# Scores from three bf16 parts on 96 rows a head, in place of two f32r parts on 96 rows for two heads

## The chip, the core and the metric

The kernel runs on one core of a Trainium2 chip. The metric is device time in microseconds of one execution, the median of the runs. Five engines work side by side: TensorE (PE, its weight loads are written PEld), VectorE (DVE), ScalarE (ACT), GpSimd (POOL) and SyncE (SP), which here only issues DMAs. They meet at semaphores; each engine works through its own list in order.

## What is computed

A transformer block on x of 2 batches x 1024 positions x 256 features: attention with 16 heads of 16 features, then a mixture of 8 low-rank maps, each with a residual and a layer norm behind it. Cut to what the change touches:

```python
Q = split_heads(Xn @ Wq + bq)
K = split_heads(Xn @ Wk + bk)
scores = jnp.einsum('bhqd,bhkd->bhqk', Q, K) / jnp.sqrt(jnp.float32(D_HEAD))
scores = jnp.where(causal, scores, jnp.float32(-jnp.inf))
A = jax.nn.softmax(scores, axis=-1)
AV = jnp.einsum('bhqk,bhkd->bhqd', A, V)
```

All inputs and outputs are float32, and the inputs are drawn so that scores are large, so q and k must enter the scores with nearly their full precision.

## The kernel before

The program is one list of events (`program_order`), and each engine walks through the list and emits its own share of every event. The list is written by hand and by a small planner (`attention_order`): for each of 2 batches, 4 groups of 4 heads, 2 chunks of 512 queries.

**Projections.** Event `qk` (one of 8 a batch: 2 chunks x 2 halves of the features x q or k): PE multiplies (L691), ACT writes the value rounded to f32r, the high part, to `qk` (L473), DVE writes value minus high, the low part (L562).

**Stacks.** Event `stack` (16 in all, one for each group and chunk): SP issues six DMAs (L388) that lay parts of q and k out in `stq` and `stk`, so that one product over 96 rows gives high x high + high x low + low x high. One `stk` tile serves two heads (`PAIRS`): the rows of the other head meet zeros in `stq`, which POOL writes once (L410, L424). There are three sets of stacks. The fourth group of a batch waits until the first group's value products have read the first set. Order on SP is order in the list: groups 1 and 2 (24 DMAs) stand in one block behind the row copy of group 0, chunk 0, and ahead of that of group 0, chunk 1.

**Maxima.** Event `max`: PE computes scores with queries on the partitions (L736), on the diagonal it adds a mask by a bf16 product (L740), DVE reduces a bank to maxima (L582). `split` makes two f32r parts of the maxima (L591 to L596), `rows` turns them on PE (L746), DVE moves them to `mrow` (L604), and SP copies them as two more rows below `stq` (L399), where `stk` has -1. So the scores proper come out with their row's maximum taken off.

**Scores and values.** Event `score`: PE computes 128 keys x up to 512 queries of one head over 98 rows (L758), ACT takes the exponential (L483), POOL clears above the diagonal (L448). Event `value` (one a step, behind four scores): eight products of 32 columns of weights (L778). A step is four scores and one `value`, with two to four maxima of a later block between them. Maxima and projections pass through 4 banks of PSUM that DVE (and ACT) free, scores through 3 banks that ACT frees.

The first scores of a chunk wait for that chunk's row copy. The residual, the layer norms and the mixture (L685, L691, L788, L823) are woven in by `program_order`.

## Time and profile before

| | us |
|---|---|
| runs | 511.52, 509.01, 509.17 |
| median | 509.17 |
| span of the profiled execution | 510.6 |
| PE busy | 454.6 (89%) |
| PEld busy | 265.5 (52%) |
| DVE busy | 324.8 (64%) |
| ACT busy | 218.8 (43%) |
| POOL busy | 71.0 (14%) |

The profile names only the span of its execution; it lies between the runs, 1.4 us above their median. Busy times of PE overlap a little, since matmuls are pipelined: from start to start is the time that one takes in a stream. L12 is line 12 of the kernel. A bracket at the end of a timeline's row is idle time of that engine ahead of it, and what ended it. The batches divide the span: layer norm and projections of batch 0 to about 43 us, its attention to about 230, projections of batch 1 and the mixture of batch 0 to about 290, attention of batch 1 to about 460, then the last mixture.

### The profile page before, as it was taken

Reading aid. Unit: us, or ns where it says so; the run is one execution under the profiler, and the core shown is the slowest. Engines: PE = TensorE matmul, PEld = TensorE weight load, DVE = VectorE, ACT = ScalarE, POOL = GpSimd, SP = SyncE. Lnnn points to the kernel's source line nnn. Section 1 sums busy time; section 2 is a strip of 40 time slices with the busy share of each in tenths; the row PEclk is TensorE's granted clock in tenths of the full one; section 3 lists DMA queues with packets and bytes.
Section 4 is the critical chain, followed back from the end, with each engine's and each line's share of the span. In section 5 each row is a group of like instructions: output and inputs, shape, how many; then the busy total and the mean of one; then the engine's idle time right before and its main releaser. Section 6 shows DMA issues by size and latency. Waiting matters only on the chain.

```text
span 510.6 us, 6947 instructions
## 1 busy us (share of the span) xinstructions
PE 454.6 (89%) x2512; PEld 265.5 (52%) x2512; DVE 324.8 (64%) x780; ACT 218.8 (43%) x470; POOL 71.0 (14%) x97
## 2 busy tenths in 40 slices
PE   0289799999999999999899995999999999999693
PEld 0145565556546554357557752555655554447352
DVE  6936588678778674526476894478868855114276
ACT  1132034666666756333421131466666757532110
POOL 9720010022011010100400010012102001010000
PEclk9999699999999999799999997699999999999897
DMA  5006990025002000000423195006100000000011
GB/s 165 0 10 108 213 161 7 3 46 83 3 0 85 2 2 1 0 1 3 117 66 62 36 168 89 1 3 112 15 1 2 3 2 1 0 1 1 0 42 42
DMA packets 13266, 21.18 MB, mean 41 GB/s; under 512 B 2352, under 2 KB 9776, under 8 KB 13232
## 3 DMA queue, kind: packets, MB, share of 16 engines
q1 hardware_dynamic: 13232, 20.73, 19.5%
q8 instruction: 20, 0.33, 0.3%
q14 instruction: 14, 0.11, 0.1%
HBM read 5.78 MB, written 2.10 MB: 15 GB/s over the span
## 4 chain that ended last, share of the span: by engine, by line
PE 77%; DVE 12%; ACT 4%; DMA 2%; issue 2%; SPq 2%; DVEq 0%; ACTq 0%
PE ps L691 24%; PE ps L758 18%; PE ps L778 15%; PE ps L736 13%; PE ps L740 3%; DVE mx L582 3%; DVE nv L521 2%; PE ps L685 2%; ACT pr L483 2%; SPq L388 1%; PE ps L788 1%; DVE st L533 1%; DMA stq<-mrow 1%; DVE x L540 1%; PE ps L823 1%
## 5 line engine op out<-in xcount | busy, mean ns | idle before, releaser
L483 ACT ACTIVATE pr<-ps 128x512 f32<-128x512 f32 (+3 forms) x384 | 171.7, 493 | 164.4 <-PE ps L758 162.6
L582 DVE TENSOR_REDUCE mx<-ps 128x1 f32<-128x512 f32 (+3 forms) x304 | 185.3, 655 | 58.9 <-PE ps L740 40.7
L758 PE MATMUL ps<-stq,stk 98*128 98x512 f32 (+3 forms) x384 | 146.0, 414 | 11.8 <-DMA stq<-mrow 6.7
L736 PE MATMUL ps<-stk,stq 96*128 96x512 f32 (+3 forms) x384 | 136.0, 391 | 3.6 <-DMA stq<-qk 1.4
L758 PEld LDWEIGHTS ps<-stq,stk 98*128 98x128 f32 x384 | 71.5, 197 | 83.2 <-ACT pr L483 44.5
L448 POOL TENSOR_SCALAR_AFFINE_SELECT pr<-pr 128x512 f32<-128x512 f32 x64 | 40.9, 639 | 359.1 <-ACT pr L483 359.1
L736 PEld LDWEIGHTS ps<-stk,stq 96*128 96x128 f32 x384 | 76.0, 200 | 14.5 <-DVE mx L582 5.5
L778 PE MATMUL ps<-pr,va 128*32 128x512 f32 (+3 forms) x768 | 83.5, 507 | 0.0
L740 PE MATMUL ps<-mask,ident_b 128*128 128x128 bf16 x256 | 58.8, 237 | 0.0
L740 PEld LDWEIGHTS ps<-mask,ident_b 128*128 128x128 bf16 x256 | 25.6, 100 | 30.9 <-issue 23.1
L691 PE MATMUL ps<-pr,w_qk 128*128 128x512 f32 x64 | 31.8, 646 | 3.8 <-ACT pr L462 3.8
L691 PE MATMUL ps<-v_t,x_t 128*128 128x512 f32 x64 | 32.0, 626 | 0.0
L691 PE MATMUL ps<-u_t,avt 128*128 128x256 f32 x128 | 30.1, 382 | 0.1
L778 PEld LDWEIGHTS ps<-pr,va 128*32 128x32 f32 x768 | 15.2, 108 | 25.9 <-issue 13.8
L650 DVE TENSOR_TENSOR avx<-ps,alpha 128x512 f32<-128x512 f32 x16 | 11.1, 691 | 25.8 <-PE ps L691 25.8
L691 PEld LDWEIGHTS ps<-u_t,avt 128*128 128x128 f32 x128 | 23.3, 190 | 3.1 <-DVE mx L582 0.4
L562 DVE SCALAR_TENSOR_TENSOR qk<-ps,cols,qk 128x512 fp32r<-128x512 f32 x16 | 11.8, 748 | 19.8 <-ACT qk L473 19.8
L473 ACT ACTIVATE qk<-ps,cols 128x512 fp32r<-128x512 f32 x16 | 11.0, 688 | 30.6 <-PE ps L691 30.6
L691 PEld LDWEIGHTS ps<-pr,w_qk 128*128 128x128 f32 x64 | 12.9, 208 | 18.8 <-issue 17.2
L685 PE MATMUL ps<-ident,pr 128*128 128x128 f32 x16 | 3.0, 348 | 21.5 <-DVE pr L540 21.5
L505 ACT ACTIVATE avt<-ps 128x512 f32<-128x512 f32 x16 | 9.5, 597 | 26.6 <-PE ps L823 26.5
L691 PE MATMUL ps<-x_t,w 128*128 128x512 f32 x32 | 16.5, 653 | 1.5 <-ACT x_t L467 0.8
(72 smaller groups left out, 340.1 us busy)
## 6 DMA issues: line engine op xcount, KB each, us to landing
stk<-qk SPq DMA_DIRECT2D x16, 256.0 KB, 3.8
stq<-qk SPq DMA_DIRECT2D x32, 128.0 KB, 3.8
x_in<-in_x SPq DMA_DIRECT2D x8, 256.0 KB, 3.5
stk<-qk SPq DMA_DIRECT2D x16, 128.0 KB, 3.7
stq<-qk SPq DMA_DIRECT2D x32, 64.0 KB, 3.1
out_y<-x SPq DMA_DIRECT2D x3, 512.0 KB, 2.9
qk<-in_x SPq DMA_DIRECT2D x2, 512.0 KB, 4.0
v_t<-in_vt SPq DMA_DIRECT2D x1, 512.0 KB, 5.8
```

The lines of the kernel that those rows point to most:

```text
L448: pool.affine_select(out=blk, in_=blk, compare_op=ALU.is_ge, fill=0.0, base=0, pattern=[[0, HPG], [1, P]], channel_multiplier=-1).then_inc ...
L473: nc.scalar.activation(qk[:, w, 0, c, m].bitcast(F32R), dve_bank(ev), ACT.Identity, bias=cols[:, 2 + w, m:m + 1]).then_inc(s_high, 1)
L483: nc.scalar.activation(probs(b, g, s)[:, j, q0 - c * CHUNK:], act_bank(ev)[:, q0 - c * CHUNK:], ACT.Exp, scale=DH ** -0.5).then_inc(s_act_ ...
L562: nc.vector.scalar_tensor_tensor(qk[:, w, 1, c, m].bitcast(F32R), dve_bank(ev), cols[:, 2 + w, m:m + 1], qk[:, w, 0, c, m], ALU.add, ALU.s ...
L582: nc.vector.tensor_reduce(dst, src, AX.X, ALU.max).then_inc(s_dve_free, 1)
L650: nc.vector.tensor_tensor(avx[:, t % 2, :].rearrange("p (e r) -> p e r", e=E), dve_bank(ev).rearrange("p (e r) -> p e r", e=E), alpha[:, t ...
L685: last = nc.tensor.transpose(bank[:, tile(i)], src[:, i, tile(k)], ident[:])
L691: last = nc.tensor.matmul(out_, lhs(k), rhs(k), start=(k == 0), stop=(k == n - 1))
L736: last = nc.tensor.matmul(bank[:, i * w:(i + 1) * w], q[0:ROWS, t // TPC, j, tile(t % TPC)], k[0:ROWS, k0 // CHUNK, j % 2, 0:w], start=Tru ...
L740: last = nc.tensor.matmul(bank[:, (i + 1) * w - P:(i + 1) * w], ident_b[:], mask[:], start=False, stop=True)
L758: nc.tensor.matmul(bank[:, q0 - c * CHUNK:], stk[stack_of(b, g)][0:ROWS + 2, kt // TPC, j % 2, tile(kt % TPC)], stq[stack_of(b, g)][0:ROWS ...
L778: last = nc.tensor.matmul(values_bank[j * VW:(j + 1) * VW, q0 - c * CHUNK:], va[:, kt, g * HPG + j, :], probs(b, g, s)[:, j, q0 - c * CHUNK:],
```

## The change

q and k are kept in three bf16 parts (high, mid, low: each the rest rounded to bf16) in `qk_raw`, and a head has its own 96 rows in `stq` and in `stk`: six products of parts of 16 features each (q high with k high, mid and low; q mid with k high and mid; q low with k high). `stk` is as large as `stq`, nothing is zero, and `PAIRS` is gone. Maxima, too, are in three bf16 parts, so the scores run over 99 rows. PE's list of products is the same in number and in shape; their operands are bf16. ACT has a new instruction for every `qk` (the mid part), POOL one (the low part), both in a new event `part`, which `with_parts` puts behind the next `qk`; DVE writes the f32 rest to a ring of three (`res`) and waits there for POOL's subtraction of three events before. POOL no longer clears `stq`. A stack takes 12 DMAs in place of six, for the same number of bytes in total.

```diff
-ROWS = 2 * 3 * DH
+TERMS, PARTS = 6, 3
+ROWS = TERMS * DH
+RES = 3
...
+def with_parts(order):
+    out, pending, age = [], None, 0
+    for ev in order:
+        if pending and ev[0] == "stack":
+            out.append(pending)
+            pending = None
+        out.append(ev)
+        age += 1
+        if pending and (ev[0] == "qk" or age > 3):
+            out.append(pending)
+            pending = None
+        if ev[0] == "qk":
+            pending, age = ("part", *ev[1:]), 0
+    return out
...
-        stq = [sb(f"stq{i}", [P, C, HPG, CHUNK], F32R) for i in range(STACKS)]
-        stk = [sb(f"stk{i}", [P, C, PAIRS, CHUNK], F32R) for i in range(STACKS)]
+        stq = [sb(f"stq{i}", [P, C, HPG, CHUNK], BF16) for i in range(STACKS)]
+        stk = [sb(f"stk{i}", [P, C, HPG, CHUNK], BF16) for i in range(STACKS)]
...
-                    sp.wait_ge(s_dve_free, n_dve["qk", b, KC - 1, c, 1])
+                    sp.wait_ge(s_low, n_part["part", b, KC - 1, c, 1])
...
-                    loads = [(k[two, c], qk[heads, 1, :, c]), (k[one, c], qk[heads, 1, 0, c])]
                     for i in range(2):
                         head = slice((2 * g + i) * DH, (2 * g + i + 1) * DH)
-                        high = qk[head, 0, 0, c].rearrange("p m s -> p (m s)").unsqueeze(1)
-                        loads += [(q[2 * i * DH:2 * (i + 1) * DH, c, 2 * i:2 * i + 2], high.to_broadcast([DH, 2, KC * CHUNK])),
-                                  (q[one.start + i * DH:one.start + (i + 1) * DH, c, 2 * i:2 * i + 2], qk[head, 0, 1, c])]
-                    for dst, src in loads:
-                        sp.dma_start(dst.bitcast(F32), src).then_inc(s_stack[stack_of(b, g)][c], 16)
+                        heads = slice(2 * i, 2 * i + 2)
+                        q_parts = parts(0, c)[head].rearrange("p n m s -> p n (m s)")
+                        k_parts = parts(1, c)[head].rearrange("p n m s -> p n (m s)")
+                        row = 0
+                        for part_of_q, parts_of_k in ((0, 3), (1, 2), (2, 1)):
+                            rows_ = slice(row, row + parts_of_k * DH)
+                            row = rows_.stop
+                            same = q_parts[:, part_of_q:part_of_q + 1].to_broadcast([DH, parts_of_k, KC * CHUNK])
+                            sp.dma_start(k[rows_, c, heads], k_parts[:, 0:parts_of_k]).then_inc(s_stack[stack_of(b, g)][c], 16)
+                            sp.dma_start(q[rows_, c, heads], same).then_inc(s_stack[stack_of(b, g)][c], 16)
...
+                if kind == "part":
+                    _, _, m, c, w = ev
+                    pool.wait_ge(s_mid, n_part[ev])
+                    pool.tensor_tensor(part(w, c, 2)[:, m], res[:, n_part[ev] % RES], part(w, c, 1)[:, m],
+                                       ALU.subtract).then_inc(s_low, 1)
...
-                    nc.scalar.activation(qk[:, w, 0, c, m].bitcast(F32R), dve_bank(ev),
+                    nc.scalar.activation(part(w, c, 0)[:, m], dve_bank(ev),
                                          ACT.Identity, bias=cols[:, 2 + w, m:m + 1]).then_inc(s_high, 1)
+                if kind == "part":
+                    _, _, m, c, w = ev
+                    act.wait_ge(s_dve_free, n_dve["qk", b, m, c, w])
+                    nc.scalar.activation(part(w, c, 1)[:, m], res[:, n_part[ev] % RES], ACT.Copy).then_inc(s_mid, 1)
...
+                    if n_high[ev] > RES:
+
+                        dve.wait_ge(s_low, n_high[ev] - RES)
                     nc.vector.scalar_tensor_tensor(
-                        qk[:, w, 1, c, m].bitcast(F32R), dve_bank(ev), cols[:, 2 + w, m:m + 1],
-                        qk[:, w, 0, c, m], ALU.add, ALU.subtract).then_inc(s_dve_free, 1)
+                        res[:, n_high[ev] % RES], dve_bank(ev), cols[:, 2 + w, m:m + 1],
+                        part(w, c, 0)[:, m], ALU.add, ALU.subtract).then_inc(s_dve_free, 1)
...
                     link(nc.vector.tensor_copy(mhl[:, c, 0], whole))
-                    nc.vector.tensor_tensor(mhl[:, c, 1], whole, mhl[:, c, 0].bitcast(F32),
-                                            ALU.subtract).then_inc(s_split, 1)
+                    link(nc.vector.tensor_tensor(mres[:], whole, mhl[:, c, 0], ALU.subtract))
+                    link(nc.vector.tensor_copy(mhl[:, c, 1], mres[:]))
+                    nc.vector.tensor_tensor(mhl[:, c, 2], mres[:], mhl[:, c, 1], ALU.subtract).then_inc(s_split, 1)
```

On SP, the last of the four stacks that stand ahead of the row copy of group 0, chunk 1 (the sixfold L388 is one stack; the row copies are L399). Before:

```order
L388 DMA stk<-qk 64x1x1024
L388 DMA stk<-qk 32x1024
L388 DMA stq<-qk 32x1x1024
L388 DMA stq<-qk 16x1024
L388 DMA stq<-qk 32x1x1024
L388 DMA stq<-qk 16x1024
L399 DMA stq<-mrow 2x16x128 x3
```

The changed kernel at the same place, the second half of that stack (six more like them stand ahead; L417 and L418 are the copies to stk and stq, L429 the row copy):

```order
L417 DMA stk<-qk_raw 48x1x1024
L418 DMA stq<-qk_raw 48x1x1024
L417 DMA stk<-qk_raw 32x1x1024
L418 DMA stq<-qk_raw 32x1x1024
L417 DMA stk<-qk_raw 16x1024
L418 DMA stq<-qk_raw 16x1024
L429 DMA stq<-mrow 3x16x128 x3
```

The row copy has moved from place 50 of SP's list to place 86, behind 48 stack copies in place of 24.

On ACT, the projections at the start of batch 0, before (L462 copies the turned input, L473 writes the high parts, L483 are the first exponentials):

```order
L462 ACTIVATE pr<-ps,cols 128x512 x2
L473 ACTIVATE qk<-ps,cols 128x512 x4
L462 ACTIVATE pr<-ps,cols 128x512 x2
L473 ACTIVATE qk<-ps,cols 128x512 x4
L483 ACTIVATE pr<-ps 128x512 x4
```

And the changed kernel there (L493, L504 and L518 answer to these; L509 writes the mid part):

```order
L493 ACTIVATE pr<-ps,cols 128x512 x2
L504 ACTIVATE qk_raw<-ps,cols 128x512 x2
L509 ACTIVATE qk_raw<-res 128x512
L504 ACTIVATE qk_raw<-ps,cols 128x512
L509 ACTIVATE qk_raw<-res 128x512
L504 ACTIVATE qk_raw<-ps,cols 128x512
L509 ACTIVATE qk_raw<-res 128x512 x2
L493 ACTIVATE pr<-ps,cols 128x512 x2
```

The last two casts of chunk 0 now stand between its projections and the turned input of chunk 1.

## Rows read from the trace of the kernel before

**Rows 1.** page, part 4: shares of the chain that ended last

```profile
PE 77%; DVE 12%; ACT 4%; DMA 2%; issue 2%; SPq 2%; DVEq 0%; ACTq 0%
```

**Rows 2.** stretches: length, busy us (instructions) of each engine, granted clock

```profile
84.00:176.00 92.00, 91.97 (x629) 51.85 (x628) 69.58 (x131) 61.10 (x136) 12.73 (x20) 1.00 0.15 31
...
328.00:413.00 85.00, 84.97 (x580) 47.91 (x579) 65.10 (x122) 56.43 (x127) 12.73 (x20) 1.00 0.11 21
```

**Rows 3.** by line and shape: count, busy us, mean ns, idle before

```profile
L758 PEld LDWEIGHTS ps<-stq,stk 98*128 98x128 f32 x384 | 71.5, 197 | 83.2 <-ACT pr L483 44.5 <-issue 21.8 <-DMA stq<-mrow 7.7
...
L740 PEld LDWEIGHTS ps<-mask,ident_b 128*128 128x128 bf16 x256 | 25.6, 100 | 30.9 <-issue 23.1
...
L440 POOL TENSOR_TENSOR x_in<-x_in,flat 128x256 f32<-128x256 f32 x16 | 11.1, 730 | 26.3 <-DMA x_in<-in_x 21.1 <-DVE pr L540 5.1
```

**Rows 4.** timeline of PE, one step: start us, length us, operation

```profile
95.70 1.06 PE L778 MATMUL ps<-pr,va 128*32 128x512 f32 x8
96.70 0.50 PE L758 MATMUL ps<-stq,stk 98*128 98x512 f32 x1
97.03 0.40 PE L736 MATMUL ps<-stk,stq 96*128 96x512 f32 x1
...
98.46 0.40 PE L758 MATMUL ps<-stq,stk 98*128 98x512 f32 x1
98.69 0.40 PE L736 MATMUL ps<-stk,stq 96*128 96x512 f32 x1
99.02 0.64 PE L778 MATMUL ps<-pr,va 128*32 128x512 f32 x4
```

**Rows 5.** timeline of SP's queue, start of batch 0

```profile
35.90 1.33 SPq L388 DMA_DIRECT2D stk<-qk  x2
...
56.11 1.26 SPq L388 DMA_DIRECT2D stk<-qk  x2
...
71.97 3.47 SPq L388 DMA_DIRECT2D stq<-qk  x4
81.33 9.38 SPq L399 DMA_DIRECT2D stq<-mrow  x2
...
110.20 1.25 SPq L388 DMA_DIRECT2D stk<-qk  x2
```

**Rows 6.** the stack copies: issue ns min/median/max

```profile
L388 SPq DMA_DIRECT2D stq<-qk x64: 590/677/1677, 37.3 to 356.5; - x64
L388 SPq DMA_DIRECT2D stk<-qk x32: 577/597/787, 35.9 to 353.0; - x32
```

**Rows 7.** timeline of SP's queue, start of batch 1

```profile
251.42 1.25 SPq L388 DMA_DIRECT2D stk<-qk  x2
...
291.92 1.43 SPq L388 DMA_DIRECT2D stk<-qk  x2
...
313.06 0.68 SPq L399 DMA_DIRECT2D stq<-mrow  x1
```

**Rows 8.** timeline of ACT, end of the first projections

```profile
34.98 1.44 ACT L462 ACTIVATE pr<-ps,cols 128x512 f32<-128x512 f32 x2
```

**Rows 9.** timeline of PE, where it resumes after copies

```profile
52.59 0.96 PE L736 MATMUL ps<-stk,stq 96*128 96x512 f32 x3 [1.40 <-DMA stq<-qk]
...
83.72 0.74 PE L758 MATMUL ps<-stq,stk 98*128 98x512 f32 x2 [0.68 <-DMA stq<-mrow]
...
92.56 1.06 PE L778 MATMUL ps<-pr,va 128*32 128x512 f32 x8
...
129.03 0.50 PE L758 MATMUL ps<-stq,stk 98*128 98x512 f32 x1
...
260.53 0.62 PE L736 MATMUL ps<-stk,stq 96*128 96x128 f32 x1
...
315.85 1.22 PE L758 MATMUL ps<-stq,stk 98*128 98x512 f32 x2 [6.06 <-DMA stq<-mrow]
...
329.73 1.07 PE L778 MATMUL ps<-pr,va 128*32 128x512 f32 x8
```

More of the change, by code:

```diff
@@ L9 @@
 F32 = mybir.dt.float32
-F32R = mybir.dt.float32r
 BF16 = mybir.dt.bfloat16
@@ L257, in block_kernel @@
         o_sb = y = x1
-        early_x, early_xh = ([qk[:, w, w, c].rearrange("p m (t d) -> p (m t) d", d=D) for c in range(C)] for w in range(2))
+        early_x, early_xh = ([qk_raw[:, w, c, 0:TPC * D].rearrange("p (t d) -> p t d", d=D) for c in range(C)] for w in range(2))
         xt = pr[2][:].rearrange("p (c k) s -> p c k s", c=C)
@@ L283, in block_kernel @@
         s_high = sem("s_high")
+        s_mid = sem("s_mid")
+        s_low = sem("s_low")
         s_stack = [[sem(f"s_stack{i}_{c}") for c in range(C)] for i in range(STACKS)]
@@ L308, in block_kernel @@
         n_causal = {ev: n + 1 for n, ev in enumerate(e for e in order if e[0] == "value" and e[3] in on_diagonal)}
-        LOADS = 16 * 6
+        LOADS = 16 * 12
         def act_bank(ev):
@@ L326, in stored, with part, parts @@
             return sum(ev[1] < b for ev in n_ln3)
+        def part(w, c, n):
+            return parts(w, c)[:, n]
+        def parts(w, c):
+            return qk_raw[:, w, c].bitcast(BF16).rearrange("p (n m s) -> p n m s", n=PARTS, m=KC)
         def stack_of(b, g):
@@ L398, in _ @@
                     sp.wait_ge(s_dve_free, n_dve[ev])
-                    sp.dma_start(stq[stack_of(b, g)][ROWS:ROWS + 2, c].bitcast(F32),
-                                 mrow[:, c, :].bitcast(F32)).then_inc(s_rows[c], 16)
+                    sp.dma_start(stq[stack_of(b, g)][ROWS:ROWS + PARTS, c], mrow[:, c, :]).then_inc(s_rows[c], 16)
                 if kind == "ln3":
@@ L409, in _ @@
             pool.memset(ident[:], 0.0).then_inc(s_ident, 1)
-            pool.memset(stq[0][0:ROWS].bitcast(F32), 0.0).then_inc(s_stack_init, 1)
             pool.wait_ge(s_ident, 1)
@@ L422, in _ @@
             pool.memset(va[:, :, :, DH:], 1.0).then_inc(s_ones, 1)
-            for i in range(1, STACKS):
-                pool.memset(stq[i][0:ROWS].bitcast(F32), 0.0).then_inc(s_stack_init, 1)
-            pool.wait_ge(s_stack_init, STACKS)
+            pool.wait_ge(s_ones, 1)
             for i in range(STACKS):
-                pool.memset(stk[i][ROWS:ROWS + 2].bitcast(F32), -1.0).then_inc(s_minus, 1)
+                pool.memset(stk[i][ROWS:ROWS + PARTS], -1.0).then_inc(s_minus, 1)
                 pool.wait_ge(s_minus, i + 1)
@@ L736, in _ @@
                         last = nc.tensor.matmul(bank[:, i * w:(i + 1) * w], q[0:ROWS, t // TPC, j, tile(t % TPC)],
-                                                k[0:ROWS, k0 // CHUNK, j % 2, 0:w], start=True, stop=not diagonal)
+                                                k[0:ROWS, k0 // CHUNK, j, 0:w], start=True, stop=not diagonal)
                         if diagonal:
@@ L745, in _ @@
                     pe.wait_ge(s_split, n_split["split", b, g, c])
-                    nc.tensor.transpose(take_dve(ev)[0:2 * HPG * TPC, 0:P],
-                                        mhl[:, c].rearrange("p a h t -> p (a h t)").bitcast(F32),
-                                        ident[:]).then_inc(s_dve_full, 1)
+                    nc.tensor.matmul(take_dve(ev)[0:PARTS * HPG * TPC, 0:P], mhl[:, c].rearrange("p a h t -> p (a h t)"),
+                                     ident_b[:], start=True, stop=True).then_inc(s_dve_full, 1)
                 if kind == "score":
@@ L757, in _ @@
                     bank = take_act(ev)
-                    nc.tensor.matmul(bank[:, q0 - c * CHUNK:], stk[stack_of(b, g)][0:ROWS + 2, kt // TPC, j % 2, tile(kt % TPC)],
-                                     stq[stack_of(b, g)][0:ROWS + 2, c, j, q0 - c * CHUNK:],
+                    nc.tensor.matmul(bank[:, q0 - c * CHUNK:], stk[stack_of(b, g)][0:ROWS + PARTS, kt // TPC, j, tile(kt % TPC)],
+                                     stq[stack_of(b, g)][0:ROWS + PARTS, c, j, q0 - c * CHUNK:],
                                      start=True, stop=True).then_inc(s_act_full, 1)
```

22 lines of the change are left out of this document (9 added, 13 removed).

## The prediction, made before the changed kernel ran

> **What bounds the kernel now.** I read the chain of waits first: TensorE (PE) holds 77% of it [rows 1]. Then the stretches: from 84 to 176 us and again from 328 to 413 us PE is busy for all of the time, at the full clock, while DVE is busy for 69.6 us of 92 and ACT for 61.1 us [rows 2]. In these 177 us PE's own stream sets the pace, and what a product costs there counts in full. The start of each batch is another matter. There the copies that build the stacks (L388) stand in SP's queue ahead of the small copy of the maxima's rows (L399), for which the first score of chunk 1 waits: SP issues 24 copies from 56.11 to 75.44 us, is then idle, and issues the L399 copy at 81.33 [rows 5]; PE goes on at 83.72 after 0.68 us of waiting [rows 9]. In batch 1 the same 24 copies run from 291.92 to 313.06 with the L399 copy right behind them [rows 7], and PE, which has waited 6.06 us, goes on at 315.85 [rows 9]. So batch 0 has 81.33 - 75.44 = 5.9 us of slack on SP, batch 1 has none.
>
> **What it adds: twelve copies for six.** The bytes are the same: before 256+128+2x128+2x64 KB a chunk, after 12 copies, 768 KB in both. SP's time goes by copies. A stk copy takes 597 ns in the median, whether it moves 256 or 128 KB (32 of them between 577 and 787 ns), and a stq copy 677 ns, with long ones up to 1677 [rows 6]. Six take 19.33/4 = 4.83 us [rows 5], 0.80 each with the gaps. For twelve the lower bound is 12 x 0.64 = 7.6 us (597 ns and the 40 ns between two), the upper 12 x 0.80 = 9.7 us. The new copies are small, so the long ones should mostly go: six stk at 0.64 and six stq at 0.70 make **8.0 us** a chunk, 3.2 more than now.
>
> **Start of batch 0.** SP starts at 35.90, when DVE is done with the last projection of chunk 0 [rows 5]. Now an ACT cast and a POOL subtraction follow. No row has this cast; ACT's nearest is 1.44 / 2 = 0.72 us a copy [rows 8], of which I take 0.65 (bounds 0.5 and 0.75). POOL's two-operand instruction takes 730 ns for 256 columns [rows 3]; for 512 I take twice that less a little, 1.4 us (bounds 0.7 and 1.5). The third cast runs where ACT now begins its copies at 34.98 [rows 8] and ends at about 35.7; behind it two subtractions queue up, so SP starts near 38.5 instead of 35.9. The Trainium skill (GPSIMD Engine Reference, 3.1) gives about 2.6 cycles an element for two inputs, which would be an estimate of 1.2 us in place of 1.4 and 0.4 us off this step; no run here shows it. From SP to PE a copy needs 2.4 us (81.33 to 83.72 [rows 5, 9]). Two casts stand ahead of chunk 1's ACT copies (L462, 34.98 [rows 8]), which moves its projections by 1.6 us, and with its own cast and subtraction SP starts that chunk at about 48.9, ends at 56.9, and PE finds it at 59.3 instead of 52.59 [rows 9]: +6.7 us. From there SP's 24 copies become 48: 56.11 + 6.7 + 4 x 8.0 = 94.8, then the L399 copy, and 2.4 us later PE goes on, at 97.3 instead of 83.72: **+13.6 us**. The faster products can't help here: PE reaches this score early and waits.
>
> **Start of batch 1.** 4 x 8.0 = 32.0 us in place of 21.1, without slack [rows 7]: **+10.9 us**.
>
> **Clock.** After batch 1's wait of 6.06 us the clock stands at 1.2 GHz for a while: from the first score behind the wait to the third value product it takes 329.73 - 315.85 = 13.88 us, where batch 0, without a wait, takes 92.56 - 83.72 = 8.84 [rows 9]. The wait in batch 0 now becomes about 7 us, so I charge the same there: **+5.0 us** (bounds 0 and 6). Batch 1 pays it already.
>
> **Between the batches.** SP starts the first stack of batch 1 at 251.42 and PE uses it at 260.53 [rows 7, 9], with 260.53 - 251.42 - 4.8 - 2.4 = 1.9 us of slack. Cast and subtraction add 2.0 and the six copies 3.2: 3.3 us late. Chunk 1's stack does likewise with some 1.5 us left over after that shift, and faster maxima between other work give perhaps 2 back: **+3 us** (1 to 5). Everything behind shifts with it.
>
> **What it removes.** The clearing of stq on POOL goes; nobody waits for it in the trace, so nothing. The f32r products and their weight loads become bf16. A load of 128 columns takes 197 ns in f32 and 100 ns in bf16 [rows 3]. In a step of 3.32 us (95.70 to 99.02) the value products take 1.00 us, and four scores, four maxima and two masks are 8x512 + 2x128 = 4352 columns, by an estimate of one a cycle at the granted 2.4 GHz 1.81 us; the nearest row for it is score to maximum without a mask, 0.23 us for 512 columns against 0.213 (98.46 to 98.69 [rows 4]). The other 0.51 us are loads that nothing covers: behind the value products score to maximum is 0.33 us (96.70 to 97.03 [rows 4]), and each mask delays the next load. With loads half as long about 0.14 us should stay, of which 0.12 is the change to the value products, as now: 2.95 us, 11% less. Steps with small tiles have more loads to a column. I take 12% of the 177 us as the bound: 21 us. But DVE's 69.6 us of 92 become 86% of what would be left, with reductions and other work falling unevenly, and only rings of 4 and 3 banks between; I take three quarters, 16 us, and 2 us more for the loads behind value products in the stretches without maxima. Against that stands the fourth stack: SP starts it at 110.20 [rows 5], 24 copies will take 16 us, the L399 copy behind them lands at 128.6, and its score, at 129.03 now [rows 9], would come due at 126.9: 1.7 us a batch. Net **-14.5 us** (-9 to -21). Not on any path: two more DVE instructions of 128x16 in the split, the third row, the f32 residual.
>
> **Sum.** 13.6 + 10.9 + 5.0 + 3.0 - 14.5 = +18.0. The profiled execution's span is 510.6 us, 1.4 above the median of the runs (509.17, 509.01 to 511.52). So 528.6 of span, **527.2 us** as a median.
>
> **Rivals.**
> *SP's time goes by bytes, or PE gains far more.* If half-size copies took half the time, a chunk would stay at 4.8 us, slack would swallow batch 0's delay, batch 1's and the clock's would vanish: +2 - 17 = -15, 494 us. Against it: 256 and 128 KB take SP the same 597 ns [rows 6]. It decides below 4 x 5.5 us. A second way to this side: PE gets so fast that DVE sets the pace, 92 us becoming 70 [rows 2], 43 us off in 177, and the sum is about -10: 499 us. The Trainium skill (TensorE: Matmul & The Clock Gate, Back-to-back issue gap) has 131 ns a product of 512 columns in a stream with loads, which would do this; at 2.4 GHz a column each cycle is 213 ns, and the 0.23 of rows 4 isn't below that. Chance of both together 7%.
> *All at its cheap end.* Copies at 0.64, POOL at 0.73, no drop of the clock, 21 us saved: 10.9 + 9.4 + 0 + 1 - 21 = 0: 509.5 us. 7%, split between no change and a small gain or loss.
> *Long copies stay.* At 0.80 each a chunk is 9.7 us: 21.8 + 17.5 + 5 + 5 - 9 = +40: 549 us. For it: six of the twelve are broadcasts from 16 partitions, and the long stq copies now are the broadcasts. 13%.
> *PE's gain is small or isn't there* (bf16 loads are not what the gaps are, or DVE's 69.6 and ACT's 61.1 us of 92 [rows 2], unevenly spread, set the steps): 0 to -6 in place of -14.5: 536 to 542 us. 15%.
> *My forecast* 58%.
>
> **How the numbers follow.** The first rival is faster, the second divides into 2% faster and 5% same, the others are slower: faster 9%, same 5%, slower 86%, with 0.5%, about what runs of this kernel can tell, as the bound. Range 511 to 544 us: it leaves out the 7% at the bottom and most of the 13% at the top.
>
> **What would show it.** Right: twelve copies a chunk in about 8 us on SP; the L399 copy of batch 0 near 95 us and directly behind the stack copies; PE idle for about 7 us before it and some 17 in batch 1; a half clock behind both; steps like 95.70 to 99.02 at 3.0 us; the 92 us stretch with maxima about 8 us shorter. Wrong if a chunk's copies take under 6 us or over 9, if steps stay at 3.3 us, or if POOL's subtraction is far from 1.4 us.

## The result: 518.8 us, 1.8% slower, and the profile after

The kernel before took 509.35 us (median of 4 runs), the changed kernel 518.83 us (518.63 to 519.50, 4 runs). The ratio is 1.018, with a 95% interval from 1.0155 to 1.0201. The profiled execution after has a span of 517.8 us, against 510.6 before: +7.2 us, where the prediction had +18.0. One run told of below is left out of its comparison: the fourth of e6 took 554.0 us, over 1.5% more than the fastest of its kernel.

The page after, part 4 (shares of the chain that ended last), answers to [rows 1]:

```profile
PE 55%; SPq 18%; DVE 12%; ACT 5%; DMA 5%; issue 3%; POOL 1%; DVEq 0%; ACTq 0%
```

PE falls from 77% to 55% and SP's queue rises from 2% to 18%. PE's waits after (who is waited for: us in total, times, longest):

```profile
PE ps L795 <- DMA stq<-mrow: 24.6, 3, 15.4
...
PE ps L774 <- DMA stq<-qk_raw: 11.5, 6, 2.7
...
PE ps L795 <- ACT pr L518: 4.2, 13, 0.4
...
PE ps L729 <- ACT avt L540: 2.8, 1, 2.8
PE ps L784 <- DVE mhl L635: 2.8, 4, 0.8
```

The first line is the score that waits for the copy of the maxima's rows; it was 0.68 and 6.06 us in [rows 9]. The second line shown are maxima that wait for copies of a stack; before there was one such wait, the 1.40 us of [rows 9]. On SP after (L417 and L418 are the stack copies, L429 the row copy) this stands behind it, to be held against [rows 5, 7]:

```profile
34.93 0.72 SPq L417 DMA_DIRECT2D stk<-qk_raw  x1
...
58.88 0.67 SPq L417 DMA_DIRECT2D stk<-qk_raw  x1
...
90.53 0.79 SPq L429 DMA_DIRECT2D stq<-mrow  x1
...
300.66 0.65 SPq L417 DMA_DIRECT2D stk<-qk_raw  x1
...
332.35 0.79 SPq L429 DMA_DIRECT2D stq<-mrow  x1
```

and PE goes on (for [rows 9]):

```profile
92.86 0.61 PE L795 MATMUL ps<-stq,stk 99*128 99x512 bf16 x1 [8.15 <-DMA stq<-mrow]
...
334.69 0.61 PE L795 MATMUL ps<-stq,stk 99*128 99x512 bf16 x1 [15.44 <-DMA stq<-mrow]
```

The 48 copies take 90.53 - 58.88 = 31.65 us in batch 0 and 332.35 - 300.66 = 31.69 in batch 1, 0.66 each, and the row copy follows them at once in both. (In the traces this copy is number 52 of SP's DMAs before and 88 after, 36 places later, as from 50 to 86.) The loads and POOL's subtraction (count | busy us, mean ns), for [rows 3]:

```profile
L795 PEld LDWEIGHTS ps<-stq,stk 99*128 99x128 bf16 x384 | 34.8, 99 | 118.1 <-ACT pr L518 52.0 <-DMA stq<-mrow 26.9 <-issue 21.1
...
L470 POOL TENSOR_TENSOR qk_raw<-res,qk_raw 128x512 bf16<-128x512 f32 x16 | 18.2, 1153 | 48.1 <-ACT qk_raw L509 48.1
```

A score's load has gone from 197 to 99 ns. Where the time went shows best when the span is cut at first scores. S(b,g)c is the first score of group g, chunk c, in batch b; each number is the difference of two such starts in PE's timeline, in us. The other kernels of the table are experiments below: reordered (`e1`), two parts (`e4`), two parts in twelve copies (`e7`), all three repairs (`e10`).

| stretch | before | after | e1 | e4 | e7 | e10 |
|---|---|---|---|---|---|---|
| 0 to S(0,0)1 | 83.7 | 92.9 | 86.3 | 80.4 | 91.7 | 78.5 |
| to S(0,1)0 | 24.1 | 23.8 | 22.9 | 21.8 | 22.5 | 21.0 |
| to S(0,3)1 | 80.4 | 74.2 | 74.2 | 72.1 | 73.7 | 74.3 |
| to S(1,0)0 | 101.7 | 107.9 | 106.2 | 98.4 | 99.7 | 101.6 |
| to S(1,0)1 | 26.0 | 35.9 | 20.7 | 20.9 | 35.9 | 21.7 |
| to S(1,1)0 | 29.2 | 24.3 | 23.7 | 20.8 | 22.6 | 21.2 |
| to S(1,3)1 | 80.4 | 74.4 | 74.4 | 72.1 | 73.7 | 74.9 |
| to the end | 85.3 | 84.4 | 84.1 | 84.0 | 84.0 | 87.4 |

From before to after the rows are +9.1, -0.3, -6.2, +6.2, +9.9, -4.9, -5.9 and -0.9. Three places lose 25 us together, the starts of the two batches and the border between them; the stretches in which PE has its data gain 18. The column of e10 is from the fastest of its runs (482.31 us, the others 485.05 to 488.87).

### The profile page after: what moved, and what is told of

It is laid out like the page before. It is cut to its first block, busy times and chain, and to the rows that moved or that the text cites. A ratio compares the mean times of both kernels' runs of the same rounds, so it can differ in the third digit from the quotient of the medians.

```text
span 517.8 us, 7111 instructions
## 1 busy us (share of the span) xinstructions
PE 423.6 (82%) x2512; PEld 210.7 (41%) x2512; DVE 326.0 (63%) x812; ACT 223.6 (43%) x486; POOL 83.6 (16%) x110
## 4 chain that ended last, share of the span: by engine, by line
PE 55%; SPq 18%; DVE 12%; ACT 5%; DMA 5%; issue 3%; POOL 1%; DVEq 0%; ACTq 0%
PE ps L729 18%; PE ps L815 12%; PE ps L795 11%; SPq L417 9%; SPq L418 9%; PE ps L774 8%; DMA stq<-qk_raw 3%; DVE mx L619 3%; ACT pr L518 2%; PE ps L723 2%; PE ps L778 2%; DVE st L568 2%; POOL qk_raw L470 1%; DMA stq<-mrow 1%; PE ps L825 1%
## 5 line engine op out<-in xcount | busy, mean ns | idle before, releaser
L518 ACT ACTIVATE pr<-ps 128x512 f32<-128x512 f32 (+3 forms) x384 | 167.6, 495 | 166.4 <-PE ps L795 164.5
L795 PE MATMUL ps<-stq,stk 99*128 99x512 bf16 (+3 forms) x384 | 118.4, 340 | 32.1 <-DMA stq<-mrow 24.6
L774 PE MATMUL ps<-stk,stq 96*128 96x512 bf16 (+3 forms) x384 | 118.6, 344 | 16.4 <-DMA stq<-qk_raw 11.5
L795 PEld LDWEIGHTS ps<-stq,stk 99*128 99x128 bf16 x384 | 34.8, 99 | 118.1 <-ACT pr L518 52.0
L774 PEld LDWEIGHTS ps<-stk,stq 96*128 96x128 bf16 x384 | 38.9, 102 | 41.3 <-DMA stq<-qk_raw 14.4
L778 PE MATMUL ps<-mask,ident_b 128*128 128x128 bf16 x256 | 52.6, 231 | 0.0
L729 PE MATMUL ps<-u_t,avt 128*128 128x256 f32 x128 | 32.7, 404 | 2.8 <-ACT avt L540 2.8
L599 DVE SCALAR_TENSOR_TENSOR res<-ps,cols,qk_raw 128x512 f32<-128x512 f32 x16 | 11.8, 748 | 22.9 <-ACT qk_raw L504 20.0
L470 POOL TENSOR_TENSOR qk_raw<-res,qk_raw 128x512 bf16<-128x512 f32 x16 | 18.2, 1153 | 48.1 <-ACT qk_raw L509 48.1
L504 ACT ACTIVATE qk_raw<-ps,cols 128x512 bf16<-128x512 f32 x16 | 11.0, 686 | 27.8 <-PE ps L729 27.8
```

Source lines behind the costliest of these rows:

```text
L470: pool.tensor_tensor(part(w, c, 2)[:, m], res[:, n_part[ev] % RES], part(w, c, 1)[:, m], ALU.subtract).then_inc(s_low, 1)
L518: nc.scalar.activation(probs(b, g, s)[:, j, q0 - c * CHUNK:], act_bank(ev)[:, q0 - c * CHUNK:], ACT.Exp, scale=DH ** -0.5).then_inc(s_act_ ...
L729: last = nc.tensor.matmul(out_, lhs(k), rhs(k), start=(k == 0), stop=(k == n - 1))
L774: last = nc.tensor.matmul(bank[:, i * w:(i + 1) * w], q[0:ROWS, t // TPC, j, tile(t % TPC)], k[0:ROWS, k0 // CHUNK, j, 0:w], start=True, s ...
L778: last = nc.tensor.matmul(bank[:, (i + 1) * w - P:(i + 1) * w], ident_b[:], mask[:], start=False, stop=True)
L795: nc.tensor.matmul(bank[:, q0 - c * CHUNK:], stk[stack_of(b, g)][0:ROWS + PARTS, kt // TPC, j, tile(kt % TPC)], stq[stack_of(b, g)][0:ROWS ...
```

## The experiments

Ratios are to runs of the kernel before made beside each group of experiments; their median was 509.9 us for e1 to e4 and 510.3 for the others. "Theory" is the prediction's account: SP pays some 0.64 us a copy, twice as many copies stand ahead of the row copy, and bf16 products repay most of it.

### e1 and e2: the row copy ahead of half of the copies

SP runs over its own order:

```diff
-            for ev in order:
+            for ev in for_sp(order):
+def for_sp(order):
+    out, held = [], []
+    for ev in order:
+        if ev[0] == "stack" and ev[2] in (1, 2) and ev[3] == 1:
+            held.append(ev)
+            continue
+        out.append(ev)
+        if ev[0] == "rows" and ev[2:] == (0, 1):
+            out += held
+            held = []
+    return out
```

> The changed kernel with one thing moved: in both batches the stack copies of chunk 1 of groups 1 and 2 (24 copies) are issued on SP behind the row copy of block (0, chunk 1), not ahead of it. Same copies, same work on every other engine. Theory (the row copy's place behind 48 copies of 0.64 us is what the starts lost): the row copy of batch 0 goes out at about 82 us, when its rows are ready, and the first score of chunk 1 starts at 84 to 85 us, not at 92.9; in batch 1 it goes out at about 316 us after 24 copies and the scores start at 318 to 320, not 334.7. Together -22 us: 497 us (490 to 503). Rival (the starts are held by the maxima and by DVE, and the copies only fill the time): the score starts move by less than 3 us each and the time stays at 513 to 519.

Measured: 495.04 us, ratio to before 0.973 (0.967 to 0.979), the expected -22 within 2 us. PE in e1, at the start of chunk 1's scores in batch 1:

```profile
310.23 0.61 PE L809 MATMUL ps<-stq,stk 99*128 99x512 bf16 x1 [0.64 <-DMA stq<-mrow]
```

The wait of 15.44 us is 0.64, and the stretch from S(1,0)0 to S(1,0)1 is 20.7 us in place of 35.9. In batch 0 the score comes at 86.3 in place of 92.9, still 1.3 to 2.3 us later than expected. Nothing was taken away, the same 192 copies of the stacks are issued: it was their place, not their presence.

> The kernel before with the same move of 12 copies behind the row copy. Theory: in batch 0 the copies are all out at 71.97 us and the row copy waits until 81.33 for its rows anyway, so nothing; in batch 1 the row copy goes out at about 307 rather than 313.06 us, so -5 us: 504 us (502 to 508). Rival (the order on SP is of no weight before or after): 509 us.

Measured: 503.90 us, ratio 0.987 (0.980 to 0.994), as expected. SP in e2 issues the row copy (L413) when its rows are ready, and not when the copies end:

```profile
308.90 0.68 SPq L413 DMA_DIRECT2D stq<-mrow  x1
```

In batch 0 the score comes 0.8 us earlier (82.9), next to nothing, as the slack of [rows 5] says. So the same move is worth 5 to 6 us before and 24 after, and with it the bf16 version is the faster one: 495.0 against 503.9.

### e3 and e7: twelve copies alone

The kernel before, each copy cut in two along the columns (m is one half of them); e7 does the same on the two-part bf16 kernel of e4:

```diff
-                    loads = [(k[two, c], qk[heads, 1, :, c]), (k[one, c], qk[heads, 1, 0, c])]
-                    for i in range(2):
+                    loads = []
+                    for m in range(KC):
+                        loads += [(k[two, c, m], qk[heads, 1, :, c, m]), (k[one, c, m], qk[heads, 1, 0, c, m])]
+                        for i in range(2):
...
-        LOADS = 16 * 6
+        LOADS = 16 * 12
```

> The kernel before with each of its 6 stack copies of a chunk cut in two along the columns: 12 copies with the bytes of 6, all float32r, nothing else changed. Theory (SP pays 0.64 us a copy, whatever its size): a chunk's copies take 7.7 us, the 48 copies ahead of the row copy 31 us in both batches, batch 0 loses about 9, batch 1 about 10, the stacks at the batch borders 3 more: 531 us (525 to 540). Rival (the time on SP goes by the bytes): the halves take half as long, 509 us (507 to 512).

Measured: 535.67 us, ratio 1.054 (1.044 to 1.064): +26, inside the expected range. The copies of e3, issue ns min/median/max:

```profile
L390 SPq DMA_DIRECT2D stq<-qk x128: 553/591/1705, 37.0 to 386.3; - x128
L390 SPq DMA_DIRECT2D stk<-qk x64: 577/595/1517, 35.6 to 383.7; - x64
```

Half the bytes of [rows 6] in each copy, and the medians are 591 and 595 ns where they were 677 and 597. PE's waits at the two starts are close to those of the changed kernel (8.15 and 15.44 us):

```profile
92.80 0.79 PE L760 MATMUL ps<-stq,stk 98*128 98x512 f32 x1 [7.14 <-DMA stq<-mrow]
...
339.62 0.80 PE L760 MATMUL ps<-stq,stk 98*128 98x512 f32 x1 [16.77 <-DMA stq<-mrow]
```

So twice as many copies of half the size bring the starts of the changed kernel. Bytes are not quite without weight: in each stack of before the two copies of 128 KB to `stq` that repeat a part for two heads are the long ones, 1.29 and 0.85 us in the median by the trace, where the copy of 256 KB to `stk` takes 0.61. At half their size, in e3 and in e4, they take 0.59. What makes them long isn't shown.

> The kernel before with two bf16 parts (16 bits of each value, zero rows and clearing kept, less exact scores) and each stack copy cut in two along the columns: 12 copies a chunk as in the changed kernel, with a quarter of before's bytes each. What separates it from the changed kernel is the third part alone: its cast and subtraction, the waits these bring, and its bytes. Theory: 12 copies cost the same here as with float32r, +26 us on the 472.4 of the two-part kernel: 498 us (492 to 504); the third part then costs the other 20 us, in the opening and between the batches. Rival (the third part is free apart from its copies): 513 to 519 us.

Measured: 505.31 us, ratio 0.990 (0.987 to 0.994), 7 more than the likeliest value and 1 outside the range. I had carried over e3's +26, but e4 stands earlier at both starts and so has more to lose: by the table +11.3 at the first start and +15.0 at the second. The third part therefore costs 518.8 - 505.3 = 13.5 us, not 20. The table says where: 8.2 us between S(0,3)1 and S(1,0)0 and 1.2 in the opening (although there e7 still clears its stacks on POOL, which the changed kernel does not; see e5), the rest in small pieces.

### e4: bf16 products alone

The kernel before with bf16 for float32r in its stacks, parts and rows of maxima; six copies, 96 + 2 rows and the clearing stay. It leaves out the third part, so its scores are less exact; the maxima are turned by a bf16 product in place of PE's transpose:

```diff
-        stq = [sb(f"stq{i}", [P, C, HPG, CHUNK], F32R) for i in range(STACKS)]
-        stk = [sb(f"stk{i}", [P, C, PAIRS, CHUNK], F32R) for i in range(STACKS)]
+        stq = [sb(f"stq{i}", [P, C, HPG, CHUNK], BF16) for i in range(STACKS)]
+        stk = [sb(f"stk{i}", [P, C, PAIRS, CHUNK], BF16) for i in range(STACKS)]
...
-        mhl = sb("mhl", [P, 2, 2, HPG, TPC], F32R)
-        mrow = sb("mrow", [2 * HPG * TPC, 2, P], F32R)
+        mhl = sb("mhl", [P, 2, 2, HPG, TPC], BF16)
+        mrow = sb("mrow", [2 * HPG * TPC, 2, P], BF16)
```

> The kernel before with its two parts of each value, its stacks, the rows of the maxima and all products on them in bf16 in place of float32r: still 6 copies a chunk, each with half the bytes, zero rows and their clearing kept, so two bf16 parts carry 16 bits of a value and not 24 (less exact scores). It is the bf16 half of the change without the copies. Theory: products of scores and maxima and their loads are worth 17 us by the stretches behind the starts; batch 0 starts as before (0.64 us a copy, half the bytes gain nothing there), batch 1 gains up to 5 us since the two copies of 1.7 us become short: 488 us (484 to 493). Rival 1 (copies go by bytes): the starts gain 8 and 10 us more, under 482. Rival 2 (bf16 products gain little and the gain seen lies elsewhere, as in the cleared POOL): 500 to 509.

Measured: 472.42 us, ratio 0.927 (0.922 to 0.933): -37 us where I had expected -21. The number lies where Rival 1 has it (under 482), but not for its reason: half the bytes don't halve a copy's time on SP. They only make the long ones of before short:

```profile
L391 SPq DMA_DIRECT2D stq<-qk_raw x64: 578/592/1700, 36.1 to 324.9; - x64
L391 SPq DMA_DIRECT2D stk<-qk_raw x32: 577/595/786, 34.7 to 322.3; - x32
```

```profile
276.10 2.50 SPq L391 DMA_DIRECT2D stq<-qk_raw  x4
```

The last line, from SP's timeline, answers to the 3.47 us for four such copies in [rows 5]. What was short is the gain of PE. One stretch with and without it, before (S(0,1)0 to S(0,3)1) and then in e4: length, busy us (instructions) of PE, PEld, DVE, ACT and POOL, granted clock, DMA share, GB/s:

```profile
107.83:188.20 80.37, 79.83 (x541) 45.41 (x537) 60.99 (x127) 52.15 (x119) 12.30 (x21) 1.00 0.16 35
```

```profile
102.24:174.36 72.12, 71.25 (x540) 31.12 (x537) 60.14 (x125) 50.20 (x119) 12.47 (x21) 1.00 0.10 27
```

At the same full clock 8.25 us of 80.4 are gone, the loads' busy time falls by 14.3 us, and DVE, busy 60.14 of 72.12, still isn't what PE waits for. The stretch ahead of it goes from 24.1 to 21.8, in batch 1 from 24.1 (e2, at the full clock) to 20.8, the one at the end from 85.3 to 84.0. Both batches together: 2 x 8.25 + 2.3 + 3.2 + 1.2 = 23 us. The spans differ by 40 (510.6 and 470.7), and the rest of it is the low clock of before in batch 1 (5.1 us), the start of batch 1 (5.0: its 24 copies, without the long ones, are out before the rows are ready), and 3.3 us each up to S(0,0)1 and up to S(1,0)0.

### e5 and e9: what POOL's fills do to DVE

e5 puts the clearing back into the changed kernel; e9 moves its fill of the rows of -1 behind the opening:

```diff
             pool.memset(ident[:], 0.0).then_inc(s_ident, 1)
+            pool.memset(stq[0][0:ROWS], 0.0).then_inc(s_stack_init, 1)
...
+            for i in range(1, STACKS):
+                pool.memset(stq[i][0:ROWS], 0.0).then_inc(s_stack_init, 1)
```

```diff
-            for i in range(STACKS):
-                pool.memset(stk[i][ROWS:ROWS + PARTS], -1.0).then_inc(s_minus, 1)
-                pool.wait_ge(s_minus, i + 1)
...
                                        ALU.subtract).then_inc(s_low, 1)
+                    if ev == ("part", 0, KC - 1, C - 1, 1):
+                        pool.wait_ge(s_low, n_part[ev])
+                        for i in range(STACKS):
+                            pool.memset(stk[i][ROWS:ROWS + PARTS], -1.0).then_inc(s_minus, 1)
+                            pool.wait_ge(s_minus, i + 1)
```

> The changed kernel with one thing put back: GpSimd clears the three query stacks ahead of everything, as before (same element counts, bf16), and SP waits for it before the first copies. Theory (while GpSimd cleared, DVE's operations of the first layer norm were held up: 8.08 us for the 4 elements of its first step, and PE's first product came at 21.5 and not at 18.3 us): the first product is 3 us later, everything behind it too, +3 us on 518.8: 522 us (520 to 524). Rival (the clearing hides behind the loads, the earlier start has another cause): 518 to 519 us.

Measured: 528.08 us, ratio 1.034 (1.026 to 1.042). The mechanism holds, the size was wrong: +9.3, not +3. DVE and POOL in the opening, before and after, and DVE and PE in e5:

```profile
6.35 8.08 DVE L521 TENSOR_SCALAR nv<-mv 128x4 f32<-128x4 f32 x1
14.47 1.83 DVE L522 TENSOR_SCALAR nv<-nv 128x4 int32<-128x4 int32 x1
16.33 1.82 DVE L523 TENSOR_SCALAR nv<-nv 128x4 int32<-128x4 int32 x1
...
7.45 6.96 POOL L424 MEMSET stq<- 96x4096 f32 x2
14.47 5.51 POOL L428 MEMSET stk<- 2x2048 f32 x3
```

```profile
6.30 1.55 DVE L556 TENSOR_SCALAR nv<-mv 128x4 f32<-128x4 f32 x1
7.88 3.53 DVE L557 TENSOR_SCALAR nv<-nv 128x4 int32<-128x4 int32 x1
11.44 3.53 DVE L558 TENSOR_SCALAR nv<-nv 128x4 int32<-128x4 int32 x1
...
4.31 10.63 POOL L454 MEMSET stk<- 3x4096 bf16 x3
```

```profile
6.26 8.17 DVE L564 TENSOR_SCALAR nv<-mv 128x4 f32<-128x4 f32 x1
...
18.10 3.53 DVE L566 TENSOR_SCALAR nv<-nv 128x4 int32<-128x4 int32 x1
...
26.42 1.94 PE L731 MATMUL ps<-ident,pr 128*128 128x128 f32 x8 [26.42 <-DVE pr L583]
```

Each of the three small operations, 0.17 us long elsewhere, ends just when a fill of POOL ends; the 8 us are three fills that follow one another without a wait between them (`va` to 7.51, then the two of `stq` to 14.41). The change took 10.5 us of clearing away and made the fill of -1 longer, from 5.51 us for the three stacks (2 rows of 2048 columns each) to 10.63 (3 rows of 4096): a fill costs by columns, and 3 rows of 4096 take as long as 96 (3.5 us). The last of the three ends at 18.15 before and at 14.97 after, and PE's first product moved by the same 3.2 us, from 21.49 to 18.30. e5 has both, the clearing and the long fill: its last one ends at 21.63, and PE starts at 26.42, 8.1 us later than after. I had reckoned with before's short fill. The Trainium skill (SBUF — State Buffer, Who interferes with whom) says that GpSimd and VectorE share a pair of SBUF ports as an exclusive lock, held for a whole instruction, and that `tensor_scalar` can run in two-port modes, which take that pair. These rows agree with a lock, except that between two fills without a wait the DVE operation did not get in. That these operations ran in a two-port mode no row shows.

> The changed kernel with one thing moved: GpSimd fills the three rows of -1 of the three key stacks (10.63 us at the start) behind its last subtraction of batch 0's opening, not ahead of the first layer norm. Theory (small VectorE operations on SBUF and GpSimd's fills hold each other up: three 4-element operations ended exactly with the three fills): the layer norm ends 8 us sooner, PE's first product comes at about 10.2 us and not at 18.3, the weights are there by 7.5 us, and all behind it moves by 8 us: 511 us (509 to 513). Rival (the overlap is by chance, or the opening then waits for something else, as the clock of PE at 1.2 GHz in its first products): 516 to 519 us.

Measured: 511.12 us, ratio 1.001 (0.9994 to 1.003), as expected to 0.1 us. DVE's first small operation in e9, with no fill beside it, and PE's first product, after and e9:

```profile
18.30 1.94 PE L723 MATMUL ps<-ident,pr 128*128 128x128 f32 x8 [18.30 <-DVE pr L575]
```

```profile
6.34 0.17 DVE L557 TENSOR_SCALAR nv<-mv 128x4 f32<-128x4 f32 x1
...
10.25 1.94 PE L724 MATMUL ps<-ident,pr 128*128 128x128 f32 x8 [10.25 <-DVE pr L576]
```

### e6: the copies on two queues

```diff
-                            sp.dma_start(k[rows_, c, heads], k_parts[:, 0:parts_of_k]).then_inc(s_stack[stack_of(b, g)][c], 16)
...
+                if kind == "stack":
+                    _, _, g, c = ev
+                    act.wait_ge(s_low, n_part["part", b, KC - 1, c, 1])
...
+                            act.dma_start(stk[stack_of(b, g)][rows_, c, 2 * i:2 * i + 2],
+                                          k_parts[:, 0:parts_of_k]).then_inc(s_stack[stack_of(b, g)][c], 16)
```

> The changed kernel with the 6 key copies of each chunk issued by ScalarE on its own queue at the stack's place in its order, the 6 query copies by SyncE as before. Theory (an issue costs its engine about 0.6 us and two queues issue side by side): SP needs 3.9 us a chunk and not 7.7, the row copy of batch 0 goes out when its rows are ready (82 us) and that of batch 1 at about 318; but ScalarE spends 15 us on 24 copies while the scores of the first block wait for their exponentials, so the first block of each batch ends about 13 us later. Both together leave the starts near where they are: 508 to 522 us, 515 the likeliest. Rival 1 (ScalarE's issues cost it nothing, only the queue): 492 to 500 us. Rival 2 (the copies share the transfer engines and two queues are no faster than one): 525 us and over.

Measured: 543.76 us (the median of the three runs compared), ratio 1.067 (1.062 to 1.073), 25 us over the changed kernel and 22 over my range. ScalarE in batch 0 of e6, SP's row copy there, and PE's longest wait:

```profile
55.85 24.91 ACTq L517 DMA_DIRECT2D stk<-qk_raw  x30
80.81 2.07 ACT L531 ACTIVATE pr<-ps 128x512 f32<-128x512 f32 x4 [26.40 <-issue]
...
123.43 12.84 ACTq L517 DMA_DIRECT2D stk<-qk_raw  x12
136.37 0.49 ACT L531 ACTIVATE pr<-ps 128x384 f32<-128x384 f32 x1 [12.56 <-issue]
```

```profile
97.72 0.79 SPq L428 DMA_DIRECT2D stq<-mrow  x1
```

```profile
PE ps L808 <- ACT pr L531: 35.3, 16, 13.2
```

Rival 1 falls: the issues hold the engine, 0.83 us a copy with SP issuing beside it, and the exponentials stand behind them. PE waits 35.3 us for these, 4.2 in the changed kernel. The time lies where Rival 2 has it (525 and over), but what Rival 2 names isn't what holds PE: SP has issued its 24 copies by 86.42 us, and the row copy goes out at 97.72, when its rows are ready. The two queues do slow each other, 0.71 and 0.83 us a copy where SP alone takes 0.66. The part that I forgot is the fourth group's stack: its 12 copies a batch hold ScalarE for 12.84 us in the middle of the scores; S(0,1)0 to S(0,2)0 takes 22.8 us there and 8.7 in the changed kernel, the same stretch of batch 1 24.8 and 8.7. These 30 us on my 515 give 545. Whether a second queue that nobody else uses would help wasn't tried.

### e8: the cast at the head of ScalarE's queue

e1, with ScalarE running over an order in which the first `part` event of batch 1 has changed places with the `avt` event behind it:

```diff
+def for_act(order):
+    out = list(order)
+    i = next(i for i, ev in enumerate(out) if ev[0] == "part" and ev[1] == 1)
...
+    out[i], out[i + 1] = out[i + 1], out[i]
+    return out
```

> The changed kernel with the copies behind the row copy (495.0 us) and one more move: on ScalarE the first cast of batch 1's middle part stands behind the copy of the transposed product avt(0, 3) and not ahead of it. Theory (the cast waits 3 us at the head of ScalarE's queue for DVE's residual, which stands behind a layer norm, and TensorE waits 2.8 us for the avt copy behind the cast): -2.5 to -3 us, 492 us (491 to 494). Rival (the border of the batches is held by something else, and the wait moves to the next product): 495 us.

Measured: 493.35 us, ratio 0.968 (0.965 to 0.971); e1 has 0.973 (0.967 to 0.979), so by the runs alone it is unclear whether e8 is faster. In the trace the wait is there in the changed kernel, on ACT and PE:

```profile
240.55 0.63 ACT L509 ACTIVATE qk_raw<-res 128x512 bf16<-128x512 f32 x1 [2.97 <-DVE res L599]
241.08 0.58 ACT L540 ACTIVATE avt<-ps 128x512 f32<-128x512 f32 x1
```

```profile
241.81 0.45 PE L729 MATMUL ps<-u_t,avt 128*128 128x256 f32 x1 [2.79 <-ACT avt L540]
```

and in e8 PE doesn't wait for avt any more; from S(0,3)1 to S(1,0)0 it takes 101.1 us in place of e1's 106.2, 2 more than expected. The stretch to the end is 5 us longer (89.0 against 84.1), in which the granted clock stands at 1.2 GHz from 452 to 459 and from 462 to 469 us, and e1's from 459 to 462. Why it falls there more often I can't say. e10 has the same move and 87.4 us there, at 1.2 GHz from 444 to 451 and from 454 to 457.

### e10 and e11: the repairs together, on both versions

e10 has the edits of e1, e8 and e9. e11 has e2's, and of POOL's fills only the first stays at the start:

```diff
-            for i in range(1, STACKS):
-                pool.memset(stq[i][0:ROWS].bitcast(F32), 0.0).then_inc(s_stack_init, 1)
...
                         pool.tensor_tensor(x_in[:, t, :], x_in[:, t, :], flat[:, D:2 * D], ALU.add).then_inc(s_bo, 1)
+                    if b == 0:
+                        for i in range(1, STACKS):
+                            pool.memset(stq[i][0:ROWS].bitcast(F32), 0.0).then_inc(s_stack_init, 1)
+                        pool.wait_ge(s_stack_init, STACKS)
+                        for i in range(STACKS):
+                            pool.memset(stk[i][ROWS:ROWS + 2].bitcast(F32), -1.0).then_inc(s_minus, 1)
+                            pool.wait_ge(s_minus, i + 1)
```

> The changed kernel with all three repairs: 24 copies behind the row copy, the cast behind the avt copy, the rows of -1 late. Theory: they are at different places and add up: 493.4 - 8 = 485 us (483 to 488). Rival (the starts are next to the bound of the first block, and what comes 8 us sooner waits 8 us later): 490 to 494 us.

Measured: 486.21 us (482.31 to 488.87), ratio 0.954 (0.950 to 0.959).

> The kernel before (two float32r parts) with the same repairs as far as they apply: 12 copies behind the row copy, and only the first query stack cleared at the start, the other two and the rows of -1 behind GpSimd's additions to x. Theory: the layer norm ends about 11 us sooner (three held operations of 11.7 us become 0.5), 503.9 - 11 = 493 us (490 to 496). Against e10 it tells what the three bf16 parts are worth once neither version is held up at the same places: about 8 us for bf16 by this sum. Rival: as above, 500 to 504 us.

Measured: 492.42 us, ratio 0.965 (0.962 to 0.969). Both sums held to 1.2 us; the gains add up. With the hold-ups nearly gone from both (e11 keeps one fill ahead, and its first product comes at 11.3 us, e10's at 10.2), the three bf16 parts are ahead by 0.965 - 0.954 = 1.1%, 6 us.

### e12: a fourth stack

e10, and:

```diff
-STACKS = 3
+STACKS = 4
...
+        if ev[0] == "stack" and ev[2] == 3:
+            fourth.append(ev)
+            continue
         out.append(ev)
+        if ev[0] == "rows" and ev[2:] == (2, 0):
+            out += fourth
+            fourth = []
```

> The kernel with all three repairs and a fourth stack buffer (the bf16 stacks leave room): the fourth group's 24 copies no longer wait on SP for the last value products of group 0 and go out right behind the row copy of block (2, chunk 0). GpSimd fills one stack more, late. Theory (the fourth stack's 16 us of copies behind group 0 hold the first maximum of group 3 and the row copy of block (1, chunk 1)): the first score of (0, 1) chunk 1 comes 9.7 us behind that of (0, 2) chunk 0, as in the two-part kernel, and not 11.4, the wait of 1.3 us at the maxima goes too: 2 to 3 us a batch, 481 us (479 to 484) against 486. Rival (these waits only take time that DVE's maxima take anyway): 485 to 487 us.

Measured: 478.63 us, ratio 0.938 (0.934 to 0.941), the fastest version with three parts, 0.4 us below the range. S(0,2)0 to S(0,1)1 takes 10.0 us (e10 11.4), S(0,1)0 to S(0,3)1 72.9 (74.3), the same in batch 1 73.0 (74.9): 3.2 us of the 7.6 between the medians. The two profiled executions differ by 3.6 (477.0 and 480.6 us of span), so the other 4 us are in runs that have no trace, and stay open. The rival's 485 to 487 is out.

## Why the prediction was right, and where its terms were off

Direction and range (511 to 544) held; the value was 8.4 us too high. Step by step, on the span:

The range held by 7.8 us at its lower end. It did not hold by errors that cancel: four of the five below lowered the time.

**Twelve copies in about 8 us: right.** 31.65 and 31.69 us for four chunks, where 32.0 stood, the row copy directly behind. e3 shows that the number of copies does it, e1 that their place ahead of the row copy does. The long copies of before went, as I had put it: 0.66 us each with the gaps.

**Start of batch 0, +13.6: measured +9.1.** The largest piece of the error is the step "the clearing goes; nobody waits for it, so nothing": 3.2 us of gain. No semaphore tied DVE to POOL, so no wait was listed, but DVE's three small operations were held all the same. With those 3.2 us added back SP starts at 38.1 us, where I had 38.5. POOL's subtraction took 1.15 us, not 1.4. The estimate from the Trainium skill (GPSIMD Engine Reference, 3.1 Elementwise — side-by-side cycle accounting), which I had put at 1.2 us (512 elements of 2.6 cycles are 1.1 us at the page's 1.2 GHz), was nearer than my row of 256 columns doubled. The last 1.3 us are in small pieces.

**Start of batch 1, +10.9: measured +9.9.** Right, and given back in full by e1. The wait of some 17 us that I had named was 15.44.

**Clock, +5.0: measured about +0.8.** The stretch behind each start, before and after, and e10, which has no long wait there (the clock is the column after POOL):

```profile
83.72:107.83 24.11, 24.11 (x165) 13.19 (x165) 17.16 (x34) 15.16 (x33) 2.47 (x4) 1.00 0.01 2
315.85:345.01 29.16, 29.16 (x164) 15.86 (x164) 17.30 (x33) 15.59 (x33) 2.46 (x4) 0.81 0.01 2
```

```profile
92.86:116.70 23.84, 23.84 (x165) 9.88 (x165) 17.17 (x37) 15.03 (x33) 2.25 (x4) 0.87 0.01 2
334.69:358.96 24.27, 24.23 (x165) 10.07 (x165) 17.63 (x37) 15.14 (x33) 2.25 (x4) 0.86 0.01 2
```

```profile
78.47:99.48 21.01, 21.01 (x164) 8.92 (x164) 16.76 (x38) 14.71 (x33) 2.25 (x4) 1.00 0.64 76
297.08:318.29 21.21, 21.17 (x164) 8.91 (x165) 17.20 (x38) 14.71 (x33) 2.25 (x4) 1.00 0.64 76
```

The clock did fall with batch 0's wait of 8.15 us (to 1.2 GHz from 88.7 us on), as foreseen, but cost 23.84 - 21.01 = 2.8 us. And in batch 1, where I had "pays it already", the kernel before paid 5.1 (29.16 against 24.07 at the full clock in e2) and the changed one pays 3.1: most of its low clock passes while PE waits. By the clock's rows PE works at 1.2 GHz for 11.2 us behind batch 1's start before (315.85 to 327.1), and for 6.1 and 6.6 us behind the two starts after (to 99.0 and to 341.3), and each time close to half of that is lost. My +5.0 had rested on before's batch 1 alone; in e3, with 7.14 us of waiting in batch 0, the stretch behind it does take 29.4 us in place of 24.1.

**Between the batches, +3: measured +6.2.** The waits that I had reckoned with came: PE waits for the copies of each of batch 1's two first stacks, before for neither:

```profile
267.17 0.23 PE L774 MATMUL ps<-stk,stq 96*128 96x128 bf16 x1 [2.60 <-DMA stq<-qk_raw]
...
286.15 0.61 PE L774 MATMUL ps<-stk,stq 96*128 96x512 bf16 x2 [1.96 <-DMA stq<-qk_raw]
```

I had the cast, the subtraction and the six more copies, but not who stands behind the new cast on ACT: it waits 2.97 us at the head of the queue, and PE 2.79 for the copy of avt behind it (e8). The longer split of the maxima (L784), which I had put on no path, has none of its four waits here: two of 0.84 and 0.83 us come shortly ahead of the scores that wait for the row copy anyway, two of 0.55 in the stretches to S(0,3)1 and S(1,3)1.

**Products, -14.5 net: measured about -19.** The single step was well told. The one of 3.32 us in [rows 4] takes 108.94 - 105.95 = 2.99 us after, where I had 2.95:

```profile
105.95 1.07 PE L815 MATMUL ps<-pr,va 128*32 128x512 f32 x8
...
108.94 0.64 PE L815 MATMUL ps<-pr,va 128*32 128x512 f32 x4
```

The step ahead of it, with 3840 columns, takes 2.74 us (from 103.21): by my estimate 1.60 us for the columns and 1.00 for the value products, which leaves 0.14 for loads, just the rest that I had put. What failed is "I take three quarters" of the bound, with DVE's load as the reason. From and to the same products, the two stretches of [rows 2] take 81.93 and 75.62 us in e4, where they take 91.83 and 85.17 before: 19.5 us, nearly the whole bound of 21, where I had 16, and of e4's 23 us another 4 lie outside them, where I had 2. After, the first of them takes 86.06, so it is 5.8 us shorter, not the 8 that I had named as a sign; some 2.8 us of the gain went to the low clock in it. The stretches with the fourth stack then give 2.1 and 2.3 us back (72.1 in e4, 74.2 and 74.4 after), where I had 1.7 a batch; e12, where this stack is early, has 72.9 and 73.0 where e10 has 74.3 and 74.9, so most of it is this stack.

The terms as measured, 9.1 + 9.9 + 0.8 + 6.2 - 19 = +7.0, stand against a measured +7.2. The +7.0 is no test of the account, since the products are what the other stretches leave over. The errors of batch 0's start (-4.5), batch 1's (-1.0), the clock (-4.2) and the products (-4.5) lowered the time together, and the border (+3.2) raised it: 11 us on the span. 2.4 of these don't reach the median, which stands 1.0 above the span after and not 1.4 below it.

## What to carry to other kernels

Count the copies on a queue before their bytes, and look at what waits at the end of the row of them: one small copy moved ahead of 24 others in each batch was worth 24 us, and decides here whether the change is a loss or a gain. When an instruction is added to an engine that works in order, write down what stands behind it when it waits, on ACT a copy that PE needs, or an exponential. And an engine without a listed wait can still be held: operations of 4 elements that take 8 us are a sign.
